# Maxima, values and scores of a cross-attention in a new order, and row maxima moved through DRAM

## The reference

```python
hidden = jnp.concatenate([context, latents], axis=1)          # 32 x 1556 x 512
q = (latents @ Wq.T).reshape(b, q_len, H, HD)                  # H = 16, HD = 96
k = (hidden @ Wk.T).reshape(b, s_len, KV, HD)                  # KV = 4
v = (hidden @ Wv.T).reshape(b, s_len, KV, HD)
...
scores = jnp.einsum('bkgqd,bksd->bkgqs', q, k) * scale
attn = jax.nn.softmax(scores.astype(jnp.float32), axis=-1)
out = jnp.einsum('bkgqs,bksd->bkgqd', attn, v)
...
x = x + out @ Wo.T
x = x + ffn(layernorm(x))        # gate over 8 experts, the two best, mean
```

## Time and profile before

| | |
|---|---|
| runs | 3865.01, 3868.02, 3875.79 us; median 3868.02 us |
| profiled execution, span | 3865.3 us |
| PE / PEld busy | 3626.6 us (94%) / 3325.6 us (86%) |
| DVE / ACT / POOL busy | 2510.2 us (65%) / 1730.9 us (45%) / 769.7 us (20%) |
| mean granted TensorE clock | 0.982 of full speed |
| one batch of `attend` | 98.34 us, 32 times |
| DMA | 240.04 MB in 302735 packets |

### The profile page before, as it was taken

The page is one execution under the profiler, slowest core; times in us unless marked ns, Lnnn a source line. Parts: engine busy times, 40 slices in busy tenths (PEclk is TensorE's granted clock), DMA queues, the critical chain, the costliest instruction groups (busy, mean ns, idle before and its releaser), DMA issues. The chain is left out here.

```text
span 3865.3 us, 66133 instructions
## 1 busy us (share of the span) xinstructions
PE 3626.6 (94%) x22164; PEld 3325.6 (86%) x22164; DVE 2510.2 (65%) x3568; ACT 1730.9 (45%) x3236; POOL 769.7 (20%) x437
## 2 busy tenths in 40 slices
PE   8989999999999999999999999999999999887999
PEld 7888888888888888888888888888888888776887
DVE  4356666666666666666666666666666666655554
ACT  3234444444444444444444444444444444423222
POOL 0132222222222222222222222222221222431000
PEclk9999999999999999999999999999999999998999
DMA  6521111111111111111111111111111111374100
GB/s 216 201 87 46 46 46 46 46 46 46 46 46 46 46 46 46 46 46 46 44 43 46 46 46 46 46 41 46 46 41 46 46 46 46 94 210 157 42 33 30
DMA packets 302735, 240.04 MB, mean 62 GB/s; under 512 B 197346, under 2 KB 263138, under 8 KB 302066
## 3 DMA queue, kind: packets, MB, share of 16 engines
q1 hardware_dynamic: 302706, 239.69, 21.3%
HBM read 184.38 MB, written 55.22 MB: 62 GB/s over the span
## 5 line engine op out<-in xcount | busy, mean ns | idle before, releaser
L724 PE MATMUL ps_proj<-wv_hi,parts 128*125 128x384 f32 x3072 | 910.1, 346 | 0.0
L661 DVE TENSOR_TENSOR probs_lo<-probs,probs_hi 125x448 fp32r<-125x448 f32 (+1 forms) x896 | 675.4, 768 | 244.9 <-ACT probs_hi L587 203.6
L130 POOL TENSOR_SCALAR parts<-raw 128x1000 fp32r<-128x1000 f32 (+1 forms) x198 | 217.7, 1099 | 2607.1 <-PE ps_proj L724 2419.8
L711 PE MATMUL ps_proj<-parts,wk_hi 128*128 128x500 f32 x2304 | 712.1, 390 | 4.7 <-DVEq L621 4.7
L724 PEld LDWEIGHTS ps_proj<-wv_hi,parts 128*125 128x125 f32 x3072 | 580.1, 192 | 3.5
L579 ACT ACTIVATE probs<-ps_scores 125x448 f32<-125x448 f32 (+1 forms) x896 | 461.9, 515 | 182.5 <-PE ps_scores L770 115.6
L571 ACT CAST values_hi<-ps_proj 125x384 fp32r<-125x384 f32 x384 | 184.0, 479 | 789.2 <-PE ps_proj L724 789.2
L724 PE MATMUL ps_proj<-wv_lo,parts 128*125 128x384 f32 x1536 | 532.0, 346 | 0.0
L790 PE MATMUL ps_attended<-probs_hi,values_hi 125*97 125x224 f32 (+1 forms) x1664 | 462.3, 278 | 64.1 <-DVE probs_lo L661 64.1
L711 PEld LDWEIGHTS ps_proj<-parts,wk_hi 128*128 128x128 f32 x2304 | 431.2, 188 | 94.8 <-DVEq L621 5.0
L587 ACT CAST probs_hi<-probs 125x448 fp32r<-125x448 f32 (+1 forms) x896 | 484.0, 540 | 27.4
(11 more groups left out here) (146 smaller groups left out, 5865.8 us busy)
## 6 DMA issues: line engine op xcount, KB each, us to landing
raw<-in_ctx SPq DMA_DIRECT2D x192, 500.0 KB, 3.5
qk_hi<-proj_out_hi SPq DMA_DIRECT2D x60, 224.0 KB, 2.0
qk_lo<-proj_out_lo SPq DMA_DIRECT2D x60, 224.0 KB, 2.2
queries_hi<-qk_hi SPq DMA_DIRECT2D x32, 336.0 KB, 3.5
queries_lo<-qk_lo SPq DMA_DIRECT2D x32, 336.0 KB, 3.5
att_t<-attended SPq DMA_DIRECT2D x128, 84.0 KB
raw<-att_t SPq DMA_DIRECT2D x7, 768.0 KB, 6.5
att<-att_t SPq DMA_DIRECT2D x7, 768.0 KB, 7.4
```

The lines of the kernel that those rows point to most:

```text
L661: dve.tensor_tensor(prs[1][0:R, u % PRING, 0:N], pr[0:R, u % PRING, 0:N], f(prs[0][0:R, u % PRING, 0:N]), ALU.subtract).then_inc(p_lo, 1)
L711: mm = pe.matmul(pproj[n % 2][:, 0:CS], w["wk"][a][:, j // 3, i * P:(i + 1) * P], ct[v][:, c, j // 3, :], start=(j == 0), stop=(j == 3 * K ...
L724: mm = pe.matmul(pproj[n % 2][0:VT, 0:KD], ct[a][:, t // VTC, j // 3, s], w["wv"][v][:, j // 3, :], start=(j == 0), stop=(j == 3 * KT - 1))
```

## The change

- The maxima are cut by key chunk. Parts 0 to 3 cover chunk 0 and parts 4 to 7 chunk 1; each takes two query halves of one kv head, 500 columns each, and its reduction gives two numbers. Parts 8 to 15 take one query half each and cover chunk 2 and the own keys, 2 by 278 columns. Parts 0 to 7 stand behind the key tiles of chunks 1 and 2 (one, two, one behind the three tiles of a chunk), parts 8 to 15 behind the halves of the first four value tiles.
- The row maximum is one reduction of 3 numbers per row and half. ACT then writes the 112 x 8 maxima, behind its cast of value tile 4, to a new DRAM buffer of 8 x 112, and behind its cast of value tile 5 waits for that transfer and loads the buffer as one row of 896 numbers into partition 96 of the queries. The negated unit matrix, the ones, `spread_max` and ACT's copy are gone; the keys' extra row is -1.
- Scores of unit 0 stand behind value tile 7, of units 1 to 4 behind tiles 8 to 11, and `weigh` of units 0 and 1 behind tiles 10 and 11, with the exponentials and low parts beside them.
- The last unit of a head contracts over 125 rows as well; the own values' tile is cleared once, beyond its 56 rows, and so adds zeros.
- SP loads the next queries before it stores the last head's result.

```diff
+EDGE = (CHUNKS - 1) * CS
+ENDS = (SL - EDGE) // 2
+EARLY_PARTS = (CHUNKS - 1) * KV
+PARTS = EARLY_PARTS + HALVES
+READY = 7
+def early_parts(c, i):
+    first = (c - 1) * KV
+    return [(0, 0), (first, first + 1), (first + 1, first + 3), (first + 3, first + 4)][i + 1 if c else 0]
...
 (SP)
-                    for h in range(KV):
+                    for h in range(KV - 1):
                         store(b, h)
                     sp.wait_ge(scores_done, b * NU + NU)
                     load_qk(b + 1)
+                    store(b, KV - 1)
...
 (ACT)
                         values(b, t)
-                        if t == NVT - 2:
-                            exp(b, 0)
-                            probs_hi(b, 0)
-                            exp(b, 1)
-                        if t == NVT - 3:
-                            act.wait_ge(mb_done, b + 1)
-                            act.copy(q[0][HD:HD + 1, :], pav[HD:HD + 1, :, 0:KV * HALF]).then_inc(mneg_done, 1)
-                    probs_hi(b, 1)
+                        if t == READY - 3:
+                            act.wait_ge(mrow_done, b + 1)
+                            act.dma_start(scratch["max"].rearrange("h q -> q h"), mrow[:],
+                                          allow_slow_non_contiguous=True).then_inc(max_stored, 16)
+                        if t == READY - 2:
+                            act.wait_ge(max_stored, b * 16 + 16)
+                            act.dma_start(f(q[0][HD:HD + 1, :]), scratch["max"].rearrange("(o h) q -> o (h q)", o=1)).then_inc(max_in_queries, 16)
+                        if t >= READY:
+                            exp(b, t - READY)
+                            probs_hi(b, t - READY)
...
 (DVE)
+                    if p < EARLY_PARTS:
+                        h = p % KV * 2
+                        dve.tensor_reduce(mpart[:, h:h + 2, p // KV:p // KV + 1], psc[0:HALF, k:k + 2, 0:CS], AX.X, ALU.max).then_inc(max_done, 1)
+                    else:
+                        h = p - EARLY_PARTS
+                        dve.tensor_reduce(mpart[:, h, CHUNKS - 1:CHUNKS], psc[0:HALF, k:k + 2, 0:ENDS], AX.XY, ALU.max).then_inc(max_done, 1)
-                    dve.tensor_tensor(mrow[:], mpart[:, :, 0], mpart[:, :, 1], ALU.max).then_inc(mrow_done, 1)
-                    dve.wait_ge(mrow_done, b + 1)
-                    for i in range(2):
-                        shape = [HALF, KV, HALF]
-                        dve.tensor_tensor(mdiag[:, i, :].rearrange("p (a b) -> p a b", a=KV),
-                                          negident[:].unsqueeze(1).broadcast_to(shape),
-                                          mrow[:, i * KV:(i + 1) * KV].unsqueeze(2).broadcast_to(shape),
-                                          ALU.mult).then_inc(mdiag_done, 1)
+                    dve.tensor_reduce(mrow[:].unsqueeze(2), mpart[:], AX.X, ALU.max).then_inc(mrow_done, 1)
...
-                            if not first and 2 <= n < 2 + G:
-                                invert_sums(b - 1, KV - 1, n - 2)
+                            if not first and n < G:
+                                invert_sums(b - 1, KV - 1, n)
+                            for p in range(*early_parts(c, i)):
+                                part_max(b, p)
...
-                        if t == NVT - 2:
-                            probs_lo(b, 0)
-                    for u in range(1, NU):
+                        if t > READY:
+                            probs_lo(b, t - READY - 1)
+                    for u in range(NVT - READY - 1, NU):
                         probs_lo(b, u)
...
 (PE)
-                def spread_max(b):
-                    pe.wait_ge(mdiag_done, 2 * b + 2)
-                    pe.wait_ge(o_copied, START + b * KV)
-                    pe.wait_ge(z_inverted, START + b * H)
-                    for i in range(2):
-                        mm = pe.matmul(pav[:, i, 0:KV * HALF], ones[:], mdiag[:, i, :], start=True, stop=True)
-                    mm.then_inc(mb_done, 1)
...
                         if u == 0 and n == 0:
-                            pe.wait_ge(mneg_done, b + 1)
+                            pe.wait_ge(max_in_queries, b * 16 + 16)
...
-                        R = VT if t < NVT else Q
-                        hi, lo = (x[0:R, u % PRING, c] for x in prs)
-                        pe.matmul(o, vt_hi[0:R, t, h], hi, start=(t == 0), stop=False)
+                        hi, lo = (x[:, u % PRING, c] for x in prs)
+                        pe.matmul(o, vt_hi[:, t, h], hi, start=(t == 0), stop=False)
...
                             project_keys(b, c, i)
+                            for p in range(*early_parts(c, i)):
+                                max_scores(b, p)
                     for t in range(NVT):
                         for part in range(2):
                             project_values(b, t, part)
-                            if 2 * t + part < PARTS:
-                                max_scores(b, 2 * t + part)
-                        if t == NVT - 3:
-                            spread_max(b)
-                        if t == NVT - 2:
-                            scores(b, 0)
-                            scores(b, 1)
-                    for u in range(2, AHEAD):
-                        scores(b, u)
-                    for u in range(NU):
+                            p = EARLY_PARTS + 2 * t + part
+                            if p < PARTS:
+                                max_scores(b, p)
+                        if t >= READY:
+                            scores(b, t - READY)
+                            if t - READY >= AHEAD:
+                                weigh(b, t - READY - AHEAD)
+                    for u in range(NVT - READY - AHEAD, NU):
...
+        "max": nc.dram_tensor("max_rows_t", (HALVES, HALF), F32, kind="Internal").ap(),
```

More of the change, by code:

```diff
@@ L502, in _ @@
                 load_qk(0)
+                sp.wait_ge(consts, 3)
                 load_v(0)
@@ L532, in _ @@
             def _(pool):
-                pool.memset(negident[:], 0.0).then_inc(cleared, 1)
-                pool.wait_ge(cleared, 1)
-                pool.affine_select(out=negident[:], in_=negident[:], compare_op=ALU.not_equal, fill=-1.0, base=0,
-                                   pattern=[[-1, HALF]], channel_multiplier=1).then_inc(consts, 1)
-                for n, ap in enumerate((ones[:], kt[1][HD:HD + 1], vt_hi[:, :, :, HD:HD + 1])):
+                pool.memset(f(vt_hi[:, NVT]), 0.0).then_inc(cleared, 1)
+                pool.memset(f(vt_lo[:, NVT]), 0.0).then_inc(cleared, 1)
+                pool.wait_ge(cleared, 2)
+                for n, (ap, value) in enumerate(((kt[1][HD:HD + 1], -1.0), (vt_hi[:, 0:NVT, :, HD:HD + 1], 1.0),
+                                                 (vt_hi[0:Q, NVT, :, HD:HD + 1], 1.0))):
+                    pool.memset(f(ap), value).then_inc(consts, 1)
                     pool.wait_ge(consts, n + 1)
-                    pool.memset(f(ap), 1.0).then_inc(consts, 1)
                 with pool.Fori(1, B) as b:
@@ L600, in _ @@
                         values(b, t)
-                        if t == NVT - 2:
-                            exp(b, 0)
-                            probs_hi(b, 0)
-                            exp(b, 1)
-                        if t == NVT - 3:
-                            act.wait_ge(mb_done, b + 1)
-                            act.copy(q[0][HD:HD + 1, :], pav[HD:HD + 1, :, 0:KV * HALF]).then_inc(mneg_done, 1)
-                    probs_hi(b, 1)
-                    for u in range(2, NU):
+                        if t == READY - 3:
[8 more added lines that the diff above has]
+                            probs_hi(b, t - READY)
+                    for u in range(NVT - READY, NU):
                         exp(b, u)
@@ L733, in max_scores @@
                         pe.wait_ge(exp_done, START + b * NU)
+                    if p % KV == 0 and p <= EARLY_PARTS:
+                        pe.wait_ge(proj_hi, b * NHI + (p // KV + 1) * 2 * KTILES)
                     pe.wait_ge(max_done, START + b * PARTS + max(p - 1, 0))
-                    h = p // 2
-                    first, N = MAXCOLS[p % 2]
                     for i in range(2):
-                        mm = pe.matmul(psc[0:HALF, 2 * (p % 2) + i, 0:N], q[0][0:HD, h * HALF:(h + 1) * HALF],
-                                       kt[0][:, h // 2, first + i * N:first + (i + 1) * N], start=True, stop=True)
-                    mm.then_inc(maxmm_done, 1)
-                def spread_max(b):
-                    pe.wait_ge(mdiag_done, 2 * b + 2)
-                    pe.wait_ge(o_copied, START + b * KV)
-                    pe.wait_ge(z_inverted, START + b * H)
-                    for i in range(2):
-                        mm = pe.matmul(pav[:, i, 0:KV * HALF], ones[:], mdiag[:, i, :], start=True, stop=True)
-                    mm.then_inc(mb_done, 1)
+                        if p < EARLY_PARTS:
+                            h, s = p % KV * 2 + i, slice(p // KV * CS, (p // KV + 1) * CS)
```

(5 more changed lines are left out.)

34 lines of the change are left out of this document (14 added, 20 removed).

## The result

| | before | after |
|---|---|---|
| median of the runs | 3867.95 us (4 runs) | 3915.77 us (4 runs, 3912.42 to 3917.15) |
| profiled execution, span | 3865.3 us | 3910.6 us |
| mean granted TensorE clock | 0.982 | 0.967 |

The ratio is 1.0115 with a 95% interval of 1.010 to 1.013: slower by 1.2%, where 3695 us and a gain of 4.5% were forecast. Between the two spans lie 45.3 us, 1.4 us for each of the 32 batches.

The account below looks back on a forecast made before the run. PE, busy for 94% of the span, was taken as the bound. Per batch -5.6 - 1.3 + 1.0 + 0.5 + 0 = -5.4 us, by 32 -173 us, took the span from 3865.3 to 3692; forecast 3695 us, range 3640 to 3750.

Parts of the forecast that it names:

- (d): Row maximum's store and load before unit 0: landings nearly hidden, stall of 0.5 us per batch, bounds 0 and 6.
- rival 1: At unit 0 the row comes 2.5 to 4 us late and the clock falls again: about 3823 us; chance 0.12.
- Rival 2: Same place, slower than before from about 4.4 us late; at 5.5 us late 3903 us; chance 0.07.
- (b): Last unit of a head: 125 rows instead of 56 remove slow matmul starts, gaining 1.3 us per batch, nothing to 1.4.
- (c): DVE beside the keys: new PE waits for reductions at parts 2 and 9, 1.0 us per batch, bounds 0 and 2.
- (e): DVE's low parts beside POOL, behind value tile 11: no gain, no loss; bounds -1.5 and +1.5 us per batch.
- (a): Spread of the maxima goes, with its wait, matmuls and the lower clock behind it: 5.6 us per batch gained.
- rival 5: Last unit of a head: 56 rows not the cause, 1.3 us less gain, 3737 us; inside the forecast's 0.66 chance.
- Rivals 3 and 4: DVE and POOL meet more, 2 us more per batch (0.10); even unit starts end low-part waits, -1.9 us (0.05).

Follow-up runs that it names:

- x3: The kernel after with the same bytes stored as 112 runs of 32 B, numbers returning in another order; 3681.96 us, ratio 0.952.
- x4: The kernel after with POOL's first third of the next context held one third longer, away from the two small transfers; 3822.84 us, ratio 0.9885.
- x1: The kernel after with both transfers kept, but the loaded row unread and asked for by PE only at the last unit; 3814.77 us, ratio 0.986.
- x9: The kernel after with only 448 of the 896 numbers stored, side by side; 3904.1 us.
- x6: x3 with the last unit of a head contracting over 56 rows again; 3715.61 us, ratio 0.961.
- x5: The kernel after with the store in runs of 32 B and the load collecting 896 single numbers in the right order; 3814.84 us, ratio 0.9865.
- x12: The kernel after with the maxima turned to 8 x 112 by a small matmul and stored as 8 runs of 448 B; 3699.92 us, ratio 0.956.

## Why the prediction was wrong

**Step (d), the two transfers, failed, and it alone turned the sign.** The cover was as laid out: 5.7 us for the landings, 5.9 in the trace from the end of the store's issue. The landings were not: the store was put at 2.7 to 3.0 us and took 8.0, the load at 2.0 to 2.3 and took 3.8 (3.6 in the median). The stall was 5.2 us per batch, in place of 0.5.

- The store was priced by the count of its pieces: 896 for 0.7 us, from the slope of the loads in the earlier trace rows. That slope holds where the pieces lie apart: at 64 B distance 896 numbers take 2.2 us, 0.8 more than the 112 runs of x3 (whose 1.4 us is also less than the 2.0 to 2.3 put under it). It left out where the pieces land. The earlier trace rows hold only pieces of 224 B and more, and the sentence "no row has 4-byte pieces going to DRAM" was the point to stop at: the rows could bound the count, not the crowding.
- "It can add up to 1.2 us" for the context transfer: held away from the small ones it gives back 2.8 us (x4), 1.3 on the store and 1.5 on the load.
- "It is late only if unit 0 is", of value tile 8, holds only for a short store. With unit 0 released, the held casts alone cost 3815 in place of 3682 us (x1). This did not decide after, where unit 0 was later still, but it is why x1 gives back only 101 us of the 234 that lie between after and x3.

**The range** took a stall of 0 to 1.5 us although the bounds of the unknown price were 0 and 6, and left the rest to rivals 1 and 2 with a chance of 0.19 together. Rival 2 is what happened in its place, its size (5.5 us late, 3903 us; measured 5.2 late, 3916) and the lower clock behind the wait. Of its condition, two landings above 10 us, 11.6 were measured. Its cause was another: it charged each of an engine's 56 numbers 80 ns more, and half as many numbers save 0.3 us (x9). That its size came so near is luck. Its chance of 0.07 was too low: the objection under rival 1, that the queries' 96 pieces per engine land in 3.5 us, spoke of the count alone. The range is also narrower than its own terms: the bounds of (b), (c) and (e) and a stall of 0 to 1.5 us add up to 3596 to 3849 us, and not to 3640 to 3750. The measured 3916 lies outside both.

**(a) The spread is gone.** The wait of 107.1 us doesn't occur in after. Its clock loss only goes where nothing waits in its place: the mean clock is 0.992 in x3 and 0.967 in after. The 5.6 us per batch were too much. The clock's 1.48 us were read from one batch; in the kernel before, 31 batches have the same idle of 3.46 us, and in 9 of them the clock stays at 1.00, as in the batch behind the one of the earlier trace rows:

```profile
756.20:760.32 4.12, 0.67 (x4) 0.49 (x4) 4.12 (x4) 0.48 (x1) 2.82 (x2) 1.00 0.42 124
760.32:762.74 2.42, 2.42 (x17) 2.42 (x16) 0.20 (x1) 1.03 (x2) 0.00 (x0) 1.00 0.00 0
```

The same 15 matmuls take 2.42 us there and 3.49 in the mean of all batches, so the clock cost 1.1 us. With 3.35 us of wait (107.1 by 32) and 0.49 from the first of the two matmuls to the next of the values, (a) is worth 4.9 us. The reduction takes 0.18 us (0.2 to 0.3 predicted) while POOL's subtraction runs beside it. The Trainium skill's rule (SBUF — State Buffer, Who interferes with whom: a reduction never contends with GpSimd) agrees.

**(b) 125 rows in place of 56.** 1.05 us per batch by x6 against x3, 1.3 predicted: right in cause, a little high in size, and rival 5 is out.

**(c) DVE beside the keys.** The reductions of 1000 numbers take 1.20 us, as predicted (1.12 to 1.24). The waits are 22.4 us, 0.7 per batch where 1.0 was taken, at parts 2 and 9 as named.

**(e) Low parts beside POOL.** 39.7 us, 1.24 per batch, against 2.0 before (64.1 by 32; the prediction's 2.07 divides by 31): a gain of 0.8 where none was taken, inside its bounds. Rivals 3 and 4, two us more and none at all, did not occur.

**The sum without (d).** -5.6 - 1.3 + 1.0 is -5.9 us per batch, or 3676 us of span; x3, where no transfer is waited for, has 3676.7. That agrees better than its terms, and is luck: with the sizes measured (-4.9, -1.05, +0.7, -0.8) it is about -6, because (a) was 0.7 too large and (e) 0.8 too small. Between after and x3 lie 233.9 us of span, 7.3 per batch. By the two busy lines PE is idle for 166.7 us of them, the wait of 5.2 per batch, and busy 67.3 us longer with the same 22100 matmuls. That is 2.1 per batch, of which the lower clock behind the wait makes 2.0.

## What to carry to other kernels

Price a small scattered store by how closely its pieces lie at the target, and not by their number or bytes: here 896 numbers took 2.2 us at 64 B distance and 8.0 us side by side, and turning the block on TensorE first (x12) cost less than the crowding. A DMA wait on an engine also holds all that is queued behind it there, so lay out both times, when the data is asked for and when the next work of that engine is. Read what a wait costs in clock from all its occurrences: one batch said 1.48 us, the mean was 1.1. And where no row shows an operation, its bounds belong in the range, even if the nearest row looks kind.

## What the hardware showed that was not expected

- 4-byte stores side by side: 8.0 us for 896 of them, 7.7 for 448, 2.2 for 896 at 64 B distance.
- Small and large transfers slow each other: 500 KB went from 3.5 to 4.8 us beside the crowded store (3.6 beside the 32 B runs), and that store from 8.0 to 6.7 with the context away.
- A load of 896 single numbers into one partition took 6.8 us in the median with the context beside it; as one row it took 3.6 beside the context and 2.1 without.
- The clock behind waits of the same length went both ways. In the kernel before, 31 idles of 3.46 us were followed by 1.00 in 9 batches and by 0.50 to 0.62 in 22. Behind the wait for the row it stayed at 1.00 in 5 of 32 batches of x4 (idles of 2.22 to 2.55 us) and in 9 of 32 of x5 (2.13 to 3.35), and fell in the others, the shortest 1.60 us long. In after (2.81 to 7.04 us) it fell in all 32. So the length of the idle alone doesn't tell which.
